# dt's two nine-row matmuls read copies at partitions 0 and 64 and are issued as one step

## The chip, the cores and the metric

The kernel runs on one core of one Trainium2 chip. The metric is the device time in microseconds (us) of one execution, given as the median of several runs. Engines are named as the profile names them: PE (TensorE matmuls), PEld (its weight loads), DVE (VectorE), ACT (ScalarE), POOL (GpSimd) and SP (SyncE, which only issues DMAs here). All data is fp32.

## The reference, cut to what matters

Two graph layers over 4096 nodes with 128 features, each followed by a residual and a layer norm:

```python
h   = relu(adj @ x @ gcn_w + gcn_b); h = layernorm(h) * ln_g + ln_b
xz  = h @ w_in;  xc, z = xz[:, :256], xz[:, 256:]
u   = silu(causal_conv4(xc) + conv_b)
dbc = u @ w_xp                                  # 8 (dt rank) + 16 (B) + 16 (C) columns
dt  = softplus(dbc[:, :8] @ w_dt + b_dt)        # 256 channels
hst = exp(dt*A) * hst + dt * B * u              # scan over 4096 steps, 256 channels x 16 states
y   = (sum_s hst*C + u*D_skip) * silu(z);  x1 = layernorm(x + y @ w_out)
# second layer: two three-layer MLPs, on adj @ x1 and on adj @ x2, merged by Wm
out = layernorm(x1 + concat(mlp1(2*adj@x1), mlp2(2*adj@x2)) @ Wm.T + bm)
```

What matters here is `dt`: a product over only eight rows (nine with the bias `b_dt` as a ninth row against a row of ones), for 256 channels, that is two groups g = 0 and 1 of 128.

## The kernel before

The 4096 nodes are cut into 8 chunks of 512. Everything is kept transposed, features on partitions and 512 nodes along the free dimension, so nearly every matmul is 128x128 weights by 128x512 moving data; in fp32 each is issued as two weight loads and two passes, and the profile counts both.

TensorE does two kinds of work. The bulk is the adjacency products: `one` blocks (adj @ [x, x2] for a chunk, into banks p_x and p_x2; one tile of a block is two matmuls, four passes) and `two` blocks (adj @ x1, one matmul or two passes a tile, into p_two, later into p_x and p_x2). Each block is 1 MB of adj, loaded by SP into a ring of four. Between the tiles stand the steps of the chain of the next chunk, in a fixed order: `gcn`, `cen`, `var`, `in_x`, `x_proj`, `dt1`, `dt0`, then `z` for the gate, `out`, and the MLP steps `mlp0` to `mlp3`.

A chunk is 16 units (one per state s) of two halves. In a unit ACT computes exp(dt*A) for both groups (L565), DVE scans both (L783) and multiplies by C (L792), and POOL makes dt*u*B two units ahead (L948) and adds the product to y (L957). `chain_steps(c)` (L115) puts TensorE's steps into halves of units: `x_proj` of chunk c+1 into the second half of unit o+4, `dt1` into the first half and `dt0` into the second half of unit o+5, with o = 7, 5, 3, 3, ... (`origin`, L110). `spread_blocks` (L145) then spreads the chunk's adjacency tiles over the 32 halves, so that each half carries the same cost, where a `one` tile costs 2, a `two` tile 1, and a step 1 or what `COST` (L142) says. The tiles keep their order; only how many stand between two steps follows from the costs. Chunk 0's own chain is issued after the ramp, with a list of filler tiles between its steps (`FILL`, L49; loop L514).

The steps in question: `x_proj` (L450) multiplies u by `wx3`, whose 128 columns are zero but for dt's eight at 0 to 7 and B's and C's from 16, so p_m holds dt's rows on partitions 0 to 7. ACT copies p_m's partitions 0 to 63 to `dbc` (L647), adding `one_row`, which is 1 on partition 8 only, and writes B's and C's rows to DRAM, from where they are spread over the partitions. `dt1` (L455) multiplies `dbc[0:9]` with the second 128 columns of `w_dt` into bank p_two, `dt0` (L459) with the first 128 into p_m. Both wait for `s_dbc`. ACT's `softplus` (L650) then takes |.| of both banks (L653) and exp and ln of the two together (L655, L657), DVE finishes dt (L832), and POOL makes dt*u (`dtu`, L965).

Other waits that the prediction speaks of: `take_rows` (L585), where ACT copies p_x and p_x2 out; the step `z`, whose two matmuls ACT copies to `gate` (L629) at unit 0; `out` at DVE's unit 3 and ACT's `x1` behind it (L663); `cen` on TensorE (L428), which waits for ACT's `hr` (L599), queued behind `x1`; and DVE's `add_sum` (L808), which adds a finished `two` sum to acc2, and for which a later sum's bank waits.

Of the kernel before, what the change touches and what calls it, by code (L numbers as in the profile page):

```python
# [5 lines left out]
ALU = mybir.AluOpType  # L6
ACT = mybir.ActivationFunctionType

P = 128
# [7 lines left out]
R = 8  # L17
# [11 lines left out]


ROW_B = 16

PACK = {}
_at = 0
# [80 lines left out]
def chain_steps(c):  # L115

    table = {}

    def put(unit, half, name, n):
        table.setdefault((unit, half), []).append((name, n))  # L120

    put(0, 1, "z", c)
    if c:
        put(2, 0, "out", c - 1)
    at = 2 if c == 0 else 3 if c == 1 else 4 if c == NC - 1 else 12
    put(at, 0, "mlp0", c)
    put(at, 1, "mlp1", c)
    put(at + 1, 0, "mlp2", c)
    put(at + 1, 1, "mlp3", c)
    if c + 1 < NC:  # L130
        o = origin(c)
        put(o, 0, "gcn", c + 1)
        put(o, 1, "cen", c + 1)
        put(o + 1, 0, "var", c + 1)
        put(o + 2, 0, "in_x", c + 1)
        put(o + 4, 1, "x_proj", c + 1)
        put(o + 5, 0, "dt1", c + 1)
        put(o + 5, 1, "dt0", c + 1)
    return table


COST = {"z": 2, "out": 2, "in_x": 2, "x_proj": 2}  # L142


def spread_blocks(c):  # L145
# [43 lines left out]
def two_layer_graph_kernel(nc, blocks, xs_d, pack_d, w_dt_d, eps1_d, eps2_d, bm_d, rows_d, out_d):  # L189
    ctx = ExitStack()  # L190
    with ctx:
# [76 lines left out]
        s_pack, s_wdt, s_consts_in = sem("s_pack"), sem("s_wdt"), sem("s_consts_in")  # L268
        s_xs = [sem(f"s_xs{i}") for i in range(NBLK)]
        s_zero, s_A = sem("s_zero"), sem("s_A")  # L270
        s_mean_w, s_cen_w, s_wx3, s_scales = (sem(n) for n in ("s_mean_w", "s_cen_w", "s_wx3", "s_scales"))
        s_gw, s_bxzp, s_wp, s_win, s_bias = (sem(n) for n in ("s_gw", "s_bxzp", "s_wp", "s_win", "s_bias"))
        s_tile = [sem(f"s_tile{i}") for i in range(JT)]
        s_blk = [sem(f"s_blk{i}") for i in range(RING)]
# [65 lines left out]
        @block.sync  # L340
        def _(sp_):
            def load(i):
                kind, m, k = LOADS[i]
                wait(sp_, s_blk_used, i - RING + 1)
                src = blocks[m, k] if kind == "one" else blocks[k, m]
                sp_.dma_start(ring[:, i % RING, :, :], src).then_inc(s_blk[i % RING], 16)

            for jt in range(JT):
                sp_.dma_start(xs[:, jt, :], xs_d[0, :, jt]).then_inc(s_tile[jt], 16)
                sp_.dma_start(ring[:, 0, jt, :], blocks[0, 0, :, jt]).then_inc(s_tile[jt], 16)  # L350
            for k in range(1, NBLK):
                sp_.dma_start(xs[:, JT * k:JT * (k + 1), :], xs_d[k]).then_inc(s_xs[k], 16)
                load(k)
                if k == 1:
                    sp_.dma_start(pack[:, :], pack_d).then_inc(s_pack, 16)
                if k == 3:
                    sp_.dma_start(w_dt[0:R + 1, :], w_dt_d).then_inc(s_wdt, 16)
                    sp_.dma_start(scale1[:, :], eps1_d).then_inc(s_consts_in, 16)
                    sp_.dma_start(scale2[:, :], eps2_d).then_inc(s_consts_in, 16)
                    sp_.dma_start(bm[:, :], bm_d).then_inc(s_consts_in, 16)  # L360
            for i in range(NBLK, len(LOADS)):
                load(i)
            for k in range(NC):
                sp_.wait_ge(s_fin, k + 1)
                sp_.dma_start(out_d[k], mb4(k % 2)).then_inc(s_out[k % 2], 16)
            for q in range(2):
                sp_.wait_ge(s_out[q], 16 * (NC // 2))

        @block.tensor
        def _(pe):  # L370
# [44 lines left out]
            def step(name, n):  # L415
# [16 lines left out]
                elif name == "in_x":  # L432
                    pe.wait_ge(s_h, n + 1)
                    pe.matmul(p_m[:, :], w_in[:, 0:P], hr[:, :], start=True, stop=True).then_inc(s_xc, 1)

                    wait(pe, s_zcopy, G * n)
                    if n >= 1:
                        pe.wait_ge(s_two_add, 1 + sums_added(n - 1, origin(n - 1) + 2) if n < NC - 1 else TURN + 1)
                    else:
                        pe.wait_ge(s_bias, 1)  # L440
                    pe.matmul(p_two[:, :], w_in[:, P:2 * P], hr[:, :], start=True, stop=True).then_inc(s_xc, 1)
                elif name == "z":

                    pe.wait_ge(s_dt, G * (n + 1))
                    wait(pe, s_res0, n)
                    pe.matmul(p_m[:, :], w_in[:, P * G:P * (G + 1)], hr[:, :], start=True, stop=True).then_inc(s_z, 1)
                    pe.wait_ge(s_two_add, 1 + min(sums_added(n, 1), TURN))
                    pe.matmul(p_two[:, :], w_in[:, P * (G + 1):P * (G + 2)], hr[:, :],
                              start=True, stop=True).then_inc(s_z, 1)
                elif name == "x_proj":  # L450
                    pe.wait_ge(s_u, G * (n + 1))
                    for g in range(G):
                        last = pe.matmul(p_m[:, :], wx3[:, g, :], u[:, g, :], start=g == 0, stop=g == G - 1)  # L453
                    last.then_inc(s_dbcp, 1)
                elif name == "dt1":  # L455
                    pe.wait_ge(s_dbc, n + 1)
                    pe.matmul(p_two[:, :], w_dt[0:R + 1, P:2 * P], dbc[0:R + 1, :],  # L457
                              start=True, stop=True).then_inc(s_dtp, 1)
                elif name == "dt0":  # L459
                    pe.wait_ge(s_dbc, n + 1)  # L460
                    pe.matmul(p_m[:, :], w_dt[0:R + 1, 0:P], dbc[0:R + 1, :],  # L461
                              start=True, stop=True).then_inc(s_dtp, 1)
                elif name == "out":
                    pe.wait_ge(s_yg, n + 1)
                    if n < NC - 1:
                        pe.wait_ge(s_zcopy, G * (n + 1) + 1)
                    else:
                        pe.wait_ge(s_res0, NC)
                    for t in range(JT):
                        for g in range(G):  # L470
                            last = pe.matmul(p_m4[:, t, :], y[:, n % 2, g, P * t:P * (t + 1)], w_out[:, g, :],
                                             start=g == 0, stop=g == G - 1)
                    last.then_inc(s_o, 1)
                elif name == "mlp0":
                    pe.wait_ge(s_ax2, n + 1)
                    if n == 0:
                        pe.wait_ge(s_zcopy, 1)
                    elif n == 1 or n == NC - 1:
                        pe.wait_ge(s_r, n)
                    else:  # L480
                        pe.wait_ge(s_dt, G * (n + 2))
                    pe.matmul(p_m[:, :], W2[:, 0, :], ax2[:, n % 2, :], start=True, stop=True).then_inc(s_mm2, 1)
                elif name in ("mlp1", "mlp2"):
                    l = int(name[3])
                    pe.wait_ge(s_mr2, L * n + l)
                    pe.matmul(p_m[:, :], W2[:, l, :], mb[:, (l - 1) % 2, :], start=True, stop=True).then_inc(s_mm2, 1)  # L486
                elif name == "mlp3":
                    pe.wait_ge(s_mr2, L * n + L)
                    for t in range(JT):
                        last = pe.matmul(p_m4[:, t, :], mb[:, 0, P * t:P * (t + 1)], Wm[:, 1, :],  # L490
                                         start=True, stop=True)
                    last.then_inc(s_mm2, 1)
# [16 lines left out]
                    pe.matmul(p_m[:, :], cen_w[:, :], hr[:, :], start=True, stop=True).then_inc(s_wp, 1)  # L509
            pe.wait_ge(s_wx3, 1)  # L510
            pe.wait_ge(s_mean_w, 1)
            pe.wait_ge(s_wdt, 16)
            tile = 0
            for name in ("gcn", "cen", "var", "in_x", "x_proj", "dt1", "dt0"):  # L514
                step(name, 0)
                for _ in range(FILL.get(name, FILL["dt"] if name == "dt0" else 0)):
                    one(NBLK + tile // JT, tile % JT, tile % JT + 1)
                    tile += 1
            assert tile == JT * len(FILL_BLOCKS)
# [38 lines left out]
        def _(act):  # L558
# [35 lines left out]
            def step(name, n):  # L594
# [47 lines left out]
                elif name == "x_proj":  # L642
# [1 line left out]
                    wait(act, s_dtp, G * n)  # L644
                    wait(act, s_rows, 16 * n)
                    wait(act, s_x1, n - 1)
                    act.activation(dbc[0:64, :], p_m[0:64, :], ACT.Identity, bias=one_row[0:64, :]).then_inc(s_dbc, 1)  # L647
                    act.wait_ge(s_dbc, n + 1)
                    act.dma_start(rows_d[b], dbc[ROW_B:ROW_B + 2 * S, :]).then_inc(s_rows, 16)
                elif name == "softplus":  # L650
# [290 lines left out]
        def _(pool):  # L941
# [18 lines left out]
            def step(name, n):  # L960
# [9 lines left out]
                elif name == "resid":  # L970
# [10 lines left out]

            pool.affine_select(out=cen_w[:, :], in_=cen_w[:, :], compare_op=ALU.not_equal, fill=1.0 - 1.0 / D,
                               base=0, pattern=[[-1, P]], channel_multiplier=1).then_inc(s_cen_w, 1)
            pool.affine_select(out=one_row[:, :], in_=one_row[:, :], compare_op=ALU.not_equal, fill=1.0,
                               base=-R, pattern=[[0, 1]], channel_multiplier=1)
            pool.memset(mean_w[:, :], 1.0 / D).then_inc(s_mean_w, 1)
            pool.memset(acc2[:, :], 0.0).then_inc(s_two_add, 1)
            pool.wait_ge(s_pack, 16)
            pool.tensor_copy(wx3[:, :, 0:R], w_xp[:, :, 0:R])
            pool.tensor_copy(wx3[:, :, ROW_B:ROW_B + S], w_xp[:, :, R:R + S])  # L990
            pool.tensor_copy(wx3[:, :, ROW_B + S:ROW_B + 2 * S], w_xp[:, :, R + S:R + 2 * S]).then_inc(s_wx3, 1)
            step("dtu", 0)
# [59 lines left out]
```

## Time and profile before

| | |
|---|---|
| median of 3 runs | 875.76 us (872.22 to 877.38) |
| the profiled execution's own time | 871.53 us |
| its span (first to last instruction) | 869.4 us |
| mean granted TensorE clock | 0.981 |
| PE busy | 830.5 us (96%), 2074 records |
| POOL, DVE, ACT busy | 639.6 (74%), 607.8 (70%), 376.2 (43%) |
| HBM | 206.65 MB read, 241 GB/s over the span |

How to read it: PE's records overlap (a pass of 512 columns has a record of 592 ns, but the next one begins 430 ns behind it), so its busy time says that it hardly pauses, not how much it does. What a step costs on PE is read from the starts of its neighbours, or from the chain of work, which cuts the records where the next begins.

### The profile page before, as it was taken

How to read it: one execution, taken by the hardware profiler on the slowest of the kernel's cores; microseconds unless marked ns; L12 is line 12 of the kernel's file. 1: busy time of each engine (PE TensorE's matmuls, PEld its weight loads, DVE VectorE, ACT ScalarE, POOL GpSimd, SP SyncE). 2: the span in 40 equal slices, each digit the busy share in tenths (PEclk: the TensorE clock that was granted, in tenths of full speed). 3: DMA queues.
4: the chain of work that ended last, by engine and by line, in shares of the span. 5: the costliest groups of instructions: out<-in, count | busy, mean ns of one | idle time of the engine just before them, and what ended most of it. 6: DMA issues, size and time to landing. Idle time of an engine off the chain costs nothing.

```text
span 869.4 us, 7245 instructions
## 1 busy us (share of the span) xinstructions
PE 830.5 (96%) x2074; PEld 374.7 (43%) x2074; DVE 607.8 (70%) x826; ACT 376.2 (43%) x605; POOL 639.6 (74%) x292
## 2 busy tenths in 40 slices
PE   7999989998999999989998999899989998999996
PEld 3444434344444444444444444444444443444453
DVE  0002187877887887888778886888688879886147
ACT  0003444546562655356434643464346536321233
POOL 2000399999899989997999799989997999991000
PEclk9999989999999999999999999999999999899998
DMA  8744567675567657865778567857788999796701
GB/s 328 304 145 142 170 208 228 204 261 199 191 202 264 219 193 283 294 244 191 257 246 276 175 247 245 290 190 246 247 327 287 333 373 353 270 400 236 282 28 73
DMA packets 59482, 209.75 MB, mean 241 GB/s; under 512 B 6954, under 2 KB 7603, under 8 KB 43059
## 3 DMA queue, kind: packets, MB, share of 16 engines
q1 hardware_dynamic: 22194, 141.65, 44.3%
q10 hardware_dynamic: 37248, 67.65, 24.1%
q8 instruction: 16, 0.26, 0.1%
q14 instruction: 24, 0.19, 0.1%
HBM read 206.65 MB, written 2.62 MB: 241 GB/s over the span
## 4 chain that ended last, share of the span: by engine, by line
PE 83%; DVE 9%; ACT 3%; issue 2%; POOL 1%; DMA 1%; ACTq 0%; DVEq 0%; SPq 0%
PE p_x L380 46%; PE p_x L399 18%; PE p_two L399 4%; DVE p_h L783 4%; PE p_m L486 2%; PE p_m L453 2%; DVE prod L792 2%; PE p_dA L555 1%; PE p_m L428 1%; DVE bn L813 1%; PE p_two L457 1%; DVE nmean L842 1%; PE p_m L461 1%; ACT x L678 1%; PE p_m L431 1%
## 5 line engine op out<-in xcount | busy, mean ns | idle before, releaser
L380 PE MATMUL p_x<-ring,xs 128*128 128x512 f32 x1024 | 459.5, 601 | 7.1 <-DMA ring<-adj_blocks 5.8
L957 POOL TENSOR_TENSOR y<-y,prod 128x1024 f32<-128x1024 f32 x127 | 298.8, 2353 | 48.6 <-DVE prod L792 48.5
L380 PEld LDWEIGHTS p_x<-ring,xs 128*128 128x128 f32 x1024 | 194.6, 192 | 255.6 <-issue 249.5
L948 POOL TENSOR_TENSOR bh<-spread,dtu 128x1024 f32<-128x1024 f32 x128 | 301.7, 2357 | 2.7 <-DMA spread<-bc_rows 2.5
L783 DVE TENSOR_TENSOR_SCAN p_h<-p_dA,state,bh 128x512 f32<-128x512 f32 x224 | 276.2, 1279 | 37.5 <-ACT p_dA L565 30.0
L565 ACT ACTIVATE p_dA<-dt,A 128x512 f32<-128x512 f32 x256 | 171.6, 689 | 144.2 <-DVE p_h L783 140.1
L399 PE MATMUL p_x<-ring,x 128*128 128x512 f32 x384 | 174.3, 605 | 2.3 <-issue 2.3
L792 DVE TENSOR_TENSOR prod<-p_h,spread_C 128x1024 f32<-128x1024 f32 x128 | 155.3, 1213 | 0.0
L399 PEld LDWEIGHTS p_x<-ring,x 128*128 128x128 f32 x384 | 73.8, 194 | 96.5 <-issue 96.5
L965 POOL TENSOR_TENSOR dtu<-dt,u 128x1024 f32<-128x1024 f32 x8 | 18.8, 2353 | 84.8 <-DVE dt L832 84.8
L399 PE MATMUL p_two<-ring,x 128*128 128x512 f32 x128 | 58.5, 592 | 0.0
L808 DVE TENSOR_TENSOR acc<-p_x,acc 128x512 f32<-128x512 f32 x32 | 21.9, 684 | 42.9 <-PE p_x L399 42.9
L783 DVE TENSOR_TENSOR_SCAN p_h<-p_dA,bh 128x512 f32<-128x512 f32 x32 | 37.5, 1218 | 13.4 <-POOL bh L948 6.2
L399 PEld LDWEIGHTS p_two<-ring,x 128*128 128x128 f32 x128 | 24.1, 190 | 29.2 <-issue 29.2
L826 DVE TENSOR_TENSOR hr<-hr,p_m 128x512 f32<-128x512 f32 x8 | 5.5, 688 | 36.8 <-ACT p_m L608 36.5
L801 DVE SCALAR_TENSOR_TENSOR p_m<-xcv,pack,p_m 128x512 f32<-128x512 f32 x24 | 18.1, 755 | 15.4 <-ACT p_m L623 14.9
L791 DVE COPY state<-p_h 128x2 f32<-128x2 f32 x128 | 19.8, 155 | 11.9 <-DMA spread_C<-bc_rows 2.5
L486 PE MATMUL p_m<-mb,pack 128*128 128x512 f32 x32 | 18.6, 666 | 9.3 <-ACT mb L684 9.3
L832 DVE SCALAR_TENSOR_TENSOR dt<-p_two,dt 128x512 f32<-128x512 f32 x8 | 5.5, 692 | 28.4 <-ACT dt L657 28.4
L589 ACT ACTIVATE ax<-p_x 128x512 f32<-128x512 f32 x8 | 4.8, 597 | 42.4 <-PE p_x L380 42.4
L684 ACT ACTIVATE mb<-p_m,pack 128x512 f32<-128x512 f32 x16 | 11.0, 689 | 24.0 <-PE p_m L486 24.0
L428 PE MATMUL p_m<-hr,cen_w 128*128 128x512 f32 x16 | 9.6, 682 | 11.4 <-ACT hr L599 11.4
(116 smaller groups left out, 552.2 us busy)
## 6 DMA issues: line engine op xcount, KB each, us to landing
ring<-adj_blocks SPq DMA_DIRECT2D x127, 1024.0 KB, 6.0
spread<-bc_rows ACTq DMA_DIRECT2D x128, 256.0 KB, 4.1
spread_C<-bc_rows ACTq DMA_DIRECT2D x128, 256.0 KB, 5.0
xs<-xs_tiles SPq DMA_DIRECT2D x7, 512.0 KB, 12.8
out_tiles<-mb SPq DMA_DIRECT2D x8, 256.0 KB, 2.0
pack<-pack_w SPq DMA_DIRECT2D x1, 1026.5 KB, 11.3
ring<-adj_blocks SPq DMA_DIRECT2D x4, 256.0 KB, 4.6
xs<-xs_tiles SPq DMA_DIRECT2D x4, 128.0 KB, 4.0
```

The costliest lines, as they stand in the source:

```text
L380: last = pe.matmul(bank[:, :], xs[:, j, D * half:D * (half + 1)], ring[:, i % RING, jt, :], start=j == 0, stop=j == N // P - 1)
L399: last = pe.matmul(sum_bank(i)[:, :], x1[:, m % KEEP, jt, :], ring[:, i % RING, jt, :], start=jt == 0 and opens(i), stop=jt == JT - 1 and ...
L428: pe.matmul(p_m[:, :], cen_w[:, :], hr[:, :], start=True, stop=True).then_inc(s_cen, 1)
L486: pe.matmul(p_m[:, :], W2[:, l, :], mb[:, (l - 1) % 2, :], start=True, stop=True).then_inc(s_mm2, 1)
L565: act.activation(p_dA[g][:, :], dt_[:, c % 2, g, :], ACT.Exp, scale=A[:, g, unit:unit + 1]).then_inc(s_dA, 1)
L783: dve.tensor_tensor_scan(p_h[:, g, :], p_dA[g][:, :], bh[:, i % 3, g, :], first, ALU.mult, ALU.add).then_inc(s_scan, 1)
L791: dve.tensor_copy(state[:, unit, :], p_h[:, :, T - 1]).then_inc(s_state, 1)
L792: dve.tensor_tensor(prod[:, i % 2, :, :], p_h[:, :, :], both(spread_C[:, i % SLOTS_C, :]), ALU.mult).then_inc(s_cmul, 1)
L808: dve.tensor_tensor(acc2[:, T * k:T * (k + 1)], sum_bank(i)[:, :], acc2[:, T * k:T * (k + 1)], ALU.add).then_inc(s_two_add, 1)
L948: pool.tensor_tensor(bh[:, i % 3, :, :], both(spread[:, i % SLOTS, :]), dtu[:, c % 2, :, :], ALU.mult).then_inc(s_bmul, 1)
L957: pool.tensor_tensor(y[:, c % 2, :, :], y[:, c % 2, :, :], prod[:, i % 2, :, :], ALU.add).then_inc(s_acc, 1)
L965: pool.tensor_tensor(dtu[:, b, :, :], dt_[:, b, :, :], u[:, :, :], ALU.mult).then_inc(s_dtu, 1)
```

## The change

`dt1` and `dt0` become one step `dt` in the first half of unit o+5 with a cost of 1 (in all 1 less per chunk than before). Its two matmuls are issued directly behind each other: group 1 reads partitions 0 to 8 of `dbc` and `w_dt`, group 0 partitions 64 to 72. For that `wx3` has dt's eight columns twice (at 0 and at 64), ACT's eviction covers all 128 partitions, `one_row` has a second one on partition 72, and `w_dt` is loaded twice. The placement of tiles by `spread_blocks` follows the new costs; the rest of the kernel is as before.

```diff
+ROW_DT = (0, 64)
...
-        put(o + 5, 0, "dt1", c + 1)
-        put(o + 5, 1, "dt0", c + 1)
+        put(o + 5, 0, "dt", c + 1)
...
-COST = {"z": 2, "out": 2, "in_x": 2, "x_proj": 2}
+COST = {"z": 2, "out": 2, "in_x": 2, "x_proj": 2, "dt": 1}
...
-                    sp_.dma_start(w_dt[0:R + 1, :], w_dt_d).then_inc(s_wdt, 16)
+                    for row in ROW_DT:
+                        sp_.dma_start(w_dt[row:row + R + 1, :], w_dt_d).then_inc(s_wdt, 16)
...
-                elif name == "dt1":
+                elif name == "dt":
+
                     pe.wait_ge(s_dbc, n + 1)
-                    pe.matmul(p_two[:, :], w_dt[0:R + 1, P:2 * P], dbc[0:R + 1, :],
-                              start=True, stop=True).then_inc(s_dtp, 1)
-                elif name == "dt0":
-                    pe.wait_ge(s_dbc, n + 1)
-                    pe.matmul(p_m[:, :], w_dt[0:R + 1, 0:P], dbc[0:R + 1, :],
-                              start=True, stop=True).then_inc(s_dtp, 1)
+                    for g, bank in ((1, p_two), (0, p_m)):
+                        rows = slice(ROW_DT[g], ROW_DT[g] + R + 1)
+                        pe.matmul(bank[:, :], w_dt[rows, P * g:P * (g + 1)], dbc[rows, :],
+                                  start=True, stop=True).then_inc(s_dtp, 1)
...
-            pe.wait_ge(s_wdt, 16)
+            pe.wait_ge(s_wdt, 32)
...
-            for name in ("gcn", "cen", "var", "in_x", "x_proj", "dt1", "dt0"):
+            for name in ("gcn", "cen", "var", "in_x", "x_proj", "dt"):
                 step(name, 0)
-                for _ in range(FILL.get(name, FILL["dt"] if name == "dt0" else 0)):
+                for _ in range(FILL[name]):
...
-                    act.activation(dbc[0:64, :], p_m[0:64, :], ACT.Identity, bias=one_row[0:64, :]).then_inc(s_dbc, 1)
+                    act.activation(dbc[:, :], p_m[:, :], ACT.Identity, bias=one_row[:, :]).then_inc(s_dbc, 1)
...
-            pool.affine_select(out=one_row[:, :], in_=one_row[:, :], compare_op=ALU.not_equal, fill=1.0,
-                               base=-R, pattern=[[0, 1]], channel_multiplier=1)
+            for q, row in enumerate(ROW_DT):
+                wait(pool, s_one_row, q)
+                pool.affine_select(out=one_row[:, :], in_=one_row[:, :], compare_op=ALU.not_equal, fill=1.0,
+                                   base=-(row + R), pattern=[[0, 1]], channel_multiplier=1).then_inc(s_one_row, 1)
...
-            pool.tensor_copy(wx3[:, :, 0:R], w_xp[:, :, 0:R])
+            for row in ROW_DT:
+                pool.tensor_copy(wx3[:, :, row:row + R], w_xp[:, :, 0:R])
```

## Rows read from the trace of the kernel before

**Rows 1.** The page, part 1: busy us, share of the span, instructions.
```profile
PE 830.5 (96%) x2074; PEld 374.7 (43%) x2074; DVE 607.8 (70%) x826; ACT 376.2 (43%) x605; POOL 639.6 (74%) x292
```

**Rows 2.** The page, part 4: the chain that ended last, by engine.
```profile
PE 83%; DVE 9%; ACT 3%; issue 2%; POOL 1%; DMA 1%; ACTq 0%; DVEq 0%; SPq 0%
```

**Rows 3.** Waits of PE: us in total, times, longest.
```profile
PE p_m L428 <- ACT hr L599: 11.4, 5, 2.5
PE p_m L486 <- ACT mb L684: 9.3, 3, 4.3
```

**Rows 4.** Stretches: engine busy us (instructions), clock, DMA; one chunk's length.
```profile
412.00:500.00 88.00, 85.55 (x212) 38.25 (x210) 70.69 (x87) 43.42 (x70) 79.49 (x35) 0.98 0.70 239
```

**Rows 5.** The chain in order of time, start us and us, around one dt.
```profile
407.10 1.72 PE p_m L453 x4
408.82 1.72 PE p_x L380 x4
410.54 1.05 PE p_two L457 x2
411.59 1.91 PE p_x L380 x4
413.50 1.05 PE p_m L461 x2
414.55 13.93 PE p_x L380 x32
```

**Rows 6.** Timeline of chunk 0's dt: start, us, instruction, [idle before <-releaser].
```profile
94.91 0.29 PEld L457 LDWEIGHTS p_two<-dbc,w_dt 9*128 9x128 f32 x2 [0.76 <-issue]
94.91 1.12 PE L457 MATMUL p_two<-dbc,w_dt 9*128 9x512 f32 x2
95.45 0.18 PEld L461 LDWEIGHTS p_m<-dbc,w_dt 9*128 9x128 f32 x1 [0.24 <-issue]
95.87 1.02 PE L461 MATMUL p_m<-dbc,w_dt 9*128 9x512 f32 x2
...
96.82 0.30 PEld L380 LDWEIGHTS p_x<-ring,xs 128*128 128x128 f32 x2 [0.76 <-issue]
...
96.93 0.60 ACT L653 ACTIVATE dt<-p_m 128x512 f32<-128x512 f32 x1 [0.26 <-PE p_m L461]
```

**Rows 7.** Timeline of chunk 1's dt, issued in chunk 0.
```profile
168.81 0.68 ACT L647 ACTIVATE dbc<-p_m,one_row 64x512 f32<-64x512 f32 x1 [3.05 <-PE p_m L453]
...
169.55 1.12 PE L457 MATMUL p_two<-dbc,w_dt 9*128 9x512 f32 x2 [0.77 <-ACT dbc L647]
```

**Rows 8.** Timeline around the step z of chunk 5.
```profile
539.31 2.35 POOL L969 TENSOR_TENSOR y<-y,gate 128x1024 f32<-128x1024 f32 x1
...
542.46 2.47 DVE L783 TENSOR_TENSOR_SCAN p_h<-p_dA,state,bh 128x512 f32<-128x512 f32 x2 [2.62 <-ACT p_dA L565]
...
544.38 1.02 PE L446 MATMUL p_m<-hr,pack 128*128 128x512 f32 x2
...
545.50 0.69 ACT L629 ACTIVATE gate<-p_m,b_xz 128x512 f32<-128x512 f32 x1 [2.56 <-PE p_m L446]
```

**Rows 9.** Timeline of chunks 6 and 7: x_proj's eviction, and waits for sums.
```profile
672.57 1.88 PE L399 MATMUL p_x<-ring,x 128*128 128x512 f32 x4
...
672.77 0.68 ACT L647 ACTIVATE dbc<-p_m,one_row 64x512 f32<-64x512 f32 x1 [1.44 <-PE p_m L453]
...
716.50 0.69 DVE L808 TENSOR_TENSOR acc<-p_x,acc 128x512 f32<-128x512 f32 x1 [2.37 <-PE p_x L399]
...
784.79 12.32 PE L399 MATMUL p_x<-ring,x 128*128 128x512 f32 x24 [2.03 <-issue]
```

**Rows 10.** The chain behind one wait of L428.
```profile
384.54 1.13 PE p_m L428 x2
385.67 3.22 PE p_x L380 x4
```

**Rows 11.** Timeline of POOL behind the kernel's start.
```profile
101.11 2.34 POOL L965 TENSOR_TENSOR dtu<-dt,u 128x1024 f32<-128x1024 f32 x1 [83.63 <-DVE dt L832]
```

More of the change, by code:

```diff
@@ L270, in two_layer_graph_kernel @@
         s_zero, s_A = sem("s_zero"), sem("s_A")
-        s_mean_w, s_cen_w, s_wx3, s_scales = (sem(n) for n in ("s_mean_w", "s_cen_w", "s_wx3", "s_scales"))
+        s_mean_w, s_cen_w, s_wx3, s_scales, s_one_row = (sem(n) for n in (
+            "s_mean_w", "s_cen_w", "s_wx3", "s_scales", "s_one_row"))
         s_gw, s_bxzp, s_wp, s_win, s_bias = (sem(n) for n in ("s_gw", "s_bxzp", "s_wp", "s_win", "s_bias"))
```

## The prediction

> **What bounds the kernel now.** I read the page's busy shares first: PE 96%, POOL 74%, DVE 70% [rows 1]. PE's records overlap, so the share alone proves nothing; the chain that ended last does: 83% of it is PE [rows 2]. Then the waits of PE: behind the start it waits for others in only two places that repeat, `cen` (L428) for ACT's `hr`, five times and 11.4 us in all, and the MLP steps (L486) for ACT, 9.3 us [rows 3]. The rest of the time it streams tiles, one pass every 0.43 us. So a microsecond that PE doesn't need is a microsecond of the kernel, if the other engines can follow. POOL is the next in line: in the 88 us of one chunk it is busy 79.5 [rows 4], 8.5 us of slack.
>
> The chain shows what one dt costs [rows 5]. Two plain tiles (four passes) take 1.72 us, so a pass takes 0.43 and a matmul of two passes 0.86. But `dt1` takes 1.05, the four passes behind it 1.91, and `dt0` 1.05 again. Entering a nine-row matmul costs 0.19 us above its passes, and so does leaving it. Rows 6 show the same in the weight loads: the first nine-row load stands 0.76 us behind the one before it instead of 0.24, likewise the first 128-row load behind the pair. Between `dt1` and `dt0`, which stand side by side there, the gap is 0.24: from one nine-row matmul to the next nothing is paid. That is a price per change between full and nine-row matmuls: four a chunk where tiles stand between the two halves of dt, two where none do.
>
> **The change part by part.** dt runs eight times: once in the prologue, and for chunks 1 to 7 inside the chunks.
>
> 1. *Two changes of shape fewer.* For chunks 1 to 7 the two matmuls now stand together, with one entry and one exit: 2 x 0.19 = 0.38 us less each [rows 5], 7 x 0.38 = 2.66 us. The prologue had them together already, nothing there. Bounds: if going from partition 0 to 64 costs as much as a change of shape, 0.19 of it stays, 1.3 us in all; above, 2.66.
>
> The Trainium skill (TensorEngine Tiling (Array Packing), Key Properties) says that changing the tiling mode drains TensorE and changing only the tile does not. The 0.19 us agree with the first half; for the second, no row here has a matmul at partition 64.
>
> 2. *The two side by side.* No row shows two matmuls at different partitions, so bounds: none of it overlaps, 0; or `dt0` vanishes wholly behind `dt1`, 0.86 us a chunk. What rows 6 show is the order: load, pass, load, pass for `dt1`, then the same for `dt0`, each pass 0.43 behind the last, in the order of issue. `dt1`'s second pass needs the same rows of the array as its first, so it can't start before the first has streamed; `dt0`'s first pass stands behind it in the queue. If order of start is kept and only the rows differ, pass 1 of `dt1` runs alone, its pass 2 beside pass 1 of `dt0`, then pass 2 of `dt0` alone: three times 0.43 instead of four. I take this middle, 0.43 us a chunk, 7 x 0.43 = 3.0 us; it is the value that the observed order of issue gives. Ends: 0 and 6.0.
>
> The Trainium skill (TensorE: Matmul & The Clock Gate, Part 3) has matmuls in different row groups start about 4 ns apart, and all of them starting and ending in program order. Read for single passes the first would hide all of `dt0`; with the second, and two passes each, one of four is hidden. No run here shows either yet.
>
> 3. *A wait in chunk 0.* TensorE waited 0.77 us for ACT's eviction there, because no tile stood between `x_proj` and `dt1` [rows 7]. Working `spread_blocks` with one less cost in the chunk, the half of `x_proj` gets one `one` tile (1.72 us), taken from the halves ahead. ACT's eviction takes 0.68 us and PE waited 0.77 for it, so a tile of 1.72 covers it: 0.77 us gained. Elsewhere the placement hardly moves: tiles shift by half a unit where no step lies between, so PE's order is the same, no sum and no `take_rows` changes its unit. Only in chunk 6 one `two` tile (0.86 us) is left between `x_proj` and `dt` instead of two. There ACT has `dbc` at 672.77 + 0.68 = 673.45 [rows 9], and with one tile less PE would reach the load at 674.38 - 0.86 = 673.52: covered by 0.07, a stall of 0 to 0.1.
>
> 4. *The prologue.* Here the chain goes from `dt` through ACT, DVE and POOL. ACT's second |.| waited 0.26 for `dt0` [rows 6]; with `dt0` 0.43 earlier that wait is gone and ACT's own first |.| is late next: 0.25 us gained, nothing if point 2 gives nothing. PE's own 0.43 there goes into its later wait at L486 (4.3 us) [rows 3].
>
> 5. *Costs.* Eviction of 128 instead of 64 partitions: 0.68 us for 64x512 in rows 7, 0.69 for 128x512 in rows 8: nothing, 0.01 a chunk at most. The second load of `w_dt`, one DMA issue on SP in the ramp ahead of the later ring loads, is hidden by the ring of four; without cover one issue, some 0.4 us. POOL's extra select and copy stand before an idle time of 83.6 us [rows 11]; uncovered they would be under 0.4. `dt0` half a unit earlier adds no wait: both matmuls wait for the same `dbc`, and behind them are only tiles, already loaded. For ACT it removes a wait of about 2.4 us in front of the second |.|, which ACT and DVE turn into idle time elsewhere, as they are not the bound there.
>
> **Does it reach the end?** A chunk's gain sits at unit 8 and must pass the gate at `z`. There ACT waits 2.56 us for PE, DVE idles 2.62, and POOL had its `gate_y` done at 541.7 for a `z` at 544.4 [rows 8]: all three are ahead of PE by more than the 0.8 us that one chunk gives, and behind the gate everything starts from there, the 2.4 us wait at L428 included, which stays as long. In chunk 6 DVE waits 2.37 us for PE's sum [rows 9], so the last gain passes too. In chunk 7 PE waits 2.03 us for a DVE sum ending at 784.79 [rows 9], but DVE's stretch starts from PE's sum, so both move.
>
> Sum: 2.66 + 3.0 + 0.77 + 0.25 = 6.7 us. The profiled execution took 871.53 us with a span of 869.4; it would take 864.8. The median of the runs is 875.76, 4.2 above it, with 872.22 to 877.38 for the three runs; the same subtraction gives 869.1.
>
> **The rivals.**
>
> *No overlap.* The matmuls are beside each other in the program but not in the array: what is left is 2.66 + 0.77 = 3.4 us, 872.4. For it: nothing in the trace overlaps two passes; fp32's two passes each may hold the array. Against: different rows and different banks leave nothing to share but the queue.
>
> *Full overlap.* `dt0` starts with `dt1`: 2.66 + 6.0 + 0.77 + 0.25 = 9.7 us, 866.1. Against it the order of issue in rows 6.
>
> *The gain is swallowed.* POOL has 8.5 us slack in a chunk, but runs without a pause for long stretches, so DVE may give back what PE gains, and PE waits longer at L428 or for sums. Then 0 to 1 us is left: 875.3. Against it the idle times at the gate.
>
> *Slower, by the clock.* Behind a wait PE sometimes runs at the lower clock: four passes took 3.22 us instead of 1.72 after the wait ending at 384.54 [rows 10], a granted clock near half, 1.5 us lost. Of the like waits some are followed by it and some are not. If the shifted times made every one of the seven waits of rows 3 fall, and half of them for eight passes, that adds 2 x 1.5 + 4 x 1.5 = 9 us, against a gain of 3.4 to 6.7: about +4, 880. It decides from three more such stretches than now without overlap, five with it. Against it: the waits keep their length, and where the fall lands looks like chance already in before.
>
> **How the numbers follow.** Half overlap 0.47, none 0.25, full 0.13, swallowed 0.08, slower 0.07. The predicted time is that of half overlap, 869.1. The range goes from below full overlap less a scatter of 2 us (864) to between none and swallowed (874). 0.5% is 4.4 us, about what a measurement of this kernel can tell from no change. Half overlap is beyond it by 2.3 us, with scatter 0.85 of its cases; full nearly always; no overlap 0.25 of its cases: 0.40 + 0.13 + 0.06, so 0.60 faster. Slower by over 0.5% 0.05. The rest, 0.35, is no change.
>
> **What would show it.** In the profile after: the first nine-row load with a gap of 0.76 and the first full load behind with the same, once a chunk instead of twice (step 1). The time from the first pass of the tile before dt to the first pass behind it: 4 x 0.43 + 0.38 = 2.1 us means no overlap, 1.7 half, 1.2 full; and in the chain the starts of the two matmuls' records (step 2). No wait of L457's successor for `dbc` at about 168 us (step 3). ACT's second |.| without a wait at 97 us (step 4). Starts of L428 and `z` earlier by about 0.8 us more in every chunk, with L428's waits still about 2.4 us each. Wrong would be: L428's waits longer by the gain; more than five stretches of doubled passes; or PE's time at dt unchanged.

## The result and the profile after

| | before | after |
|---|---|---|
| median of the runs | 875.89 us (871.96 to 877.48, 6 runs) | 862.43 us (861.4 to 867.19, 6 runs) |
| profiled execution: time, span | 871.53, 869.4 | 861.8, 859.8 |
| mean granted clock | 0.981 | 0.987 |

The ratio is 0.9863, 95% interval [0.9829, 0.9896]. It goes with the means of the runs, 863.1 and 875.1 us, which lie 12.0 us apart; the medians lie 13.5 us apart, the two profiled executions 9.7. The forecast was 869.1 with a range of 864.0 to 874.0, so the kernel came out faster than its lower end.

The page of after, parts 1 and 4 (busy shares; the chain by engine), as in [rows 1, 2]: the bound is still PE.

```profile
PE 817.4 (95%) x2074; PEld 371.2 (43%) x2074; DVE 609.6 (71%) x826; ACT 374.5 (44%) x605; POOL 639.7 (74%) x294
...
PE 82%; DVE 10%; ACT 3%; issue 2%; POOL 1%; DMA 1%; ACTq 0%; DVEq 0%; SPq 0%
```

One thing first on which partitions are which. In the line `rows = slice(ROW_DT[g], ...)` with `ROW_DT = (0, 64)`, it is group 1, issued first and into p_two, that reads partitions 64 to 72, and group 0 that reads 0 to 8; the description of the change has the two the other way round. The two groups of rows differ either way, so the argument stands.

The chain of after around the dt whose counterpart stands in [rows 5] (start us, us):

```profile
405.64 1.72 PE p_m L455 x4
407.36 1.72 PE p_x L382 x4
409.07 0.62 PE p_two L462
409.70 0.01 PE p_m L462
409.70 0.42 PE p_two L462
410.12 0.01 PE p_m L462
410.13 15.65 PE p_x L382 x36
```

The whole of dt takes 0.62 + 0.01 + 0.42 + 0.01 = 1.06 us ahead of the next tile, where before it took 1.05 twice and 0.19 in the tile between: 1.23 us less (1.24 by the rounded terms of the prediction, 0.86 + 0.38). The timeline of an earlier dt of after shows why (start, us, instruction, [idle]):

```profile
247.70 0.18 PEld L462 LDWEIGHTS p_two<-dbc,w_dt 9*128 9x128 f32 x1 [0.76 <-issue]
247.70 0.69 PE L462 MATMUL p_two<-dbc,w_dt 9*128 9x512 f32 x1
247.71 0.18 PEld L462 LDWEIGHTS p_m<-dbc,w_dt 9*128 9x128 f32 x1
247.71 0.69 PE L462 MATMUL p_m<-dbc,w_dt 9*128 9x512 f32 x1
247.81 0.18 PEld L462 LDWEIGHTS p_two<-dbc,w_dt 9*128 9x128 f32 x1
247.81 0.18 PEld L462 LDWEIGHTS p_m<-dbc,w_dt 9*128 9x128 f32 x1
248.23 0.59 PE L462 MATMUL p_two<-dbc,w_dt 9*128 9x512 f32 x1
248.24 0.59 PE L462 MATMUL p_m<-dbc,w_dt 9*128 9x512 f32 x1
248.76 0.30 PEld L382 LDWEIGHTS p_x<-ring,xs 128*128 128x128 f32 x2 [0.76 <-issue]
```

Both first passes start within 0.01 us, both second passes too: `dt0` vanishes wholly behind `dt1`, its weight loads included. The gap of 0.76 us stands once ahead of the pair and once behind it; between partition 64 and partition 0 there is none. The start-to-start distance from the first pass of the pair to the first load behind it is 1.06 us, for `dt1` alone it was 674.38 to 675.43, 1.05.

Where the time went by chunk. The figures are the distances between the starts of successive `x_proj` steps, in us:

| from x_proj of chunk | 0 | 1 | 2 | 3 | 4 | 5 | 6 |
|---|---|---|---|---|---|---|---|
| before | 77.22 | 75.75 | 75.76 | 88.54 | 88.56 | 86.84 | 88.51 |
| after | 73.96 | 79.93 | 75.73 | 85.58 | 85.55 | 85.56 | 85.58 |

From chunk 3 on, after needs 85.57 each time. Before needs 86.84 once, 1.27 more: the 1.23 of the chain, 0.20 by a shorter wait of L428 (2.43 us there, 2.23 in after), less 0.16, because in after two passes of tiles take 0.51 and 0.50 us from start to start instead of 0.43 (those begun at 449.3 and 449.8 us, and at 534.8 and 535.3). And before needs about 88.54 three times, another 1.7 more. Chunk 0 gave 3.3: the 1.23, the wait of 0.77, and a low-clock stretch less (1.7), against another wait that is 0.5 longer. Chunk 2 gave nothing and chunk 1 lost 4.2. Both remainders are what the experiments are about. First the 1.7. These rows of before are the stretches behind two of the waits of L428 (columns: stretch, length, busy us of PE, PEld, DVE, ACT, POOL, granted clock, DMA share, GB/s):

```profile
386.00:390.00 4.00, 4.00 (x7) 1.73 (x6) 2.75 (x3) 1.52 (x4) 4.00 (x3) 0.61 0.65 242
...
474.00:478.00 4.00, 4.00 (x7) 1.62 (x6) 3.28 (x3) 1.79 (x3) 4.00 (x3) 0.57 0.71 262
```

And the same places of after, behind the same step:

```profile
384.00:388.00 4.00, 3.23 (x8) 1.55 (x9) 3.29 (x5) 2.51 (x5) 4.00 (x3) 1.00 0.84 310
470.00:474.00 4.00, 3.67 (x9) 1.76 (x10) 3.29 (x6) 2.06 (x4) 4.00 (x3) 1.00 0.87 322
556.00:560.00 4.00, 4.00 (x10) 1.85 (x11) 3.29 (x5) 2.16 (x4) 4.00 (x2) 1.00 0.82 299
642.00:646.00 4.00, 4.00 (x11) 1.85 (x10) 3.29 (x5) 2.56 (x5) 4.00 (x3) 1.00 0.81 309
```

Before had three stretches at the lower of the two clock levels (1.2 instead of 2.4 GHz) behind its four waits of L428 in chunks 3 to 6, each worth 1.7 us (88.54 against 86.84); after had none there. In chunk 1 it was the other way round: after had two such stretches behind a wait of L487 (208.9 us), before had none; with a wait 1.9 us longer (2.82 us) that makes the 4.2 lost, less what the pair gave. That wait was longer because of one small DVE instruction, seen here in before, and then in after:

```profile
205.97 0.17 DVE L842 TENSOR_SCALAR nmean<-mv 128x4 f32<-128x4 f32 x1
...
202.67 2.35 POOL L958 TENSOR_TENSOR y<-y,prod 128x1024 f32<-128x1024 f32 x1
202.95 2.09 DVE L843 TENSOR_SCALAR nmean<-mv 128x4 f32<-128x4 f32 x1
```

It makes four columns and lasts 2.09 us, until POOL's instruction ends (205.02). In before it took 0.17 at this place, because it fell where POOL's instruction was just ending. It stands between the statistics and x1, and so ahead of `hr` and of the waits of L428 and L487 (L430 and L487 in after, L428 and L486 in before). The wait in chunk 1 follows it: 0.91 us in before, 2.82 in after; in e1, e8 and e4 nmean takes 1.53, 1.99 and 2.22 us there and the wait lasts 2.25, 2.72 and 2.95.

### The profile page after: what moved, and what is told of

Same layout as the page of the kernel before. It is cut to its first block, busy times and chain, and to the rows that moved or that the text cites. A ratio compares the mean times of both kernels' runs of the same rounds, so it can differ in the third digit from the quotient of the medians.

```text
span 859.8 us, 7249 instructions
## 1 busy us (share of the span) xinstructions
PE 817.4 (95%) x2074; PEld 371.2 (43%) x2074; DVE 609.6 (71%) x826; ACT 374.5 (44%) x605; POOL 639.7 (74%) x294
## 4 chain that ended last, share of the span: by engine, by line
PE 82%; DVE 10%; ACT 3%; issue 2%; POOL 1%; DMA 1%; ACTq 0%; DVEq 0%; SPq 0%
PE p_x L382 46%; PE p_x L401 18%; PE p_two L401 4%; DVE p_h L784 4%; PE p_m L487 2%; PE p_m L455 2%; DVE prod L793 2%; PE p_dA L556 1%; DVE nmean L843 1%; DVE bn L814 1%; PE p_two L462 1%; PE p_m L430 1%; ACT x L679 1%; PE p_m L491 1%; PE p_m L433 1%
## 5 line engine op out<-in xcount | busy, mean ns | idle before, releaser
L401 PE MATMUL p_x<-ring,x 128*128 128x512 f32 x384 | 172.0, 600 | 3.6 <-issue 3.6
L487 PE MATMUL p_m<-mb,pack 128*128 128x512 f32 x32 | 19.4, 693 | 11.7 <-ACT mb L685 11.7
L802 DVE SCALAR_TENSOR_TENSOR p_m<-xcv,pack,p_m 128x512 f32<-128x512 f32 x24 | 18.1, 755 | 15.4 <-ACT p_m L624 14.8
L809 DVE TENSOR_TENSOR acc<-p_two,acc 128x512 f32<-128x512 f32 x8 | 5.5, 685 | 22.7 <-PE p_two L401 22.7
L430 PE MATMUL p_m<-hr,cen_w 128*128 128x512 f32 x16 | 8.7, 625 | 11.7 <-ACT hr L600 11.7
```

Source lines behind the costliest of these rows:

```text
L401: last = pe.matmul(sum_bank(i)[:, :], x1[:, m % KEEP, jt, :], ring[:, i % RING, jt, :], start=jt == 0 and opens(i), stop=jt == JT - 1 and ...
L802: dve.scalar_tensor_tensor(out=bank[:, :], in0=xcv[:, g, k:k + T], scalar=conv_w[:, g, k:k + 1], in1=bank[:, :], op0=ALU.mult, op1=ALU.add ...
L809: dve.tensor_tensor(acc2[:, T * k:T * (k + 1)], sum_bank(i)[:, :], acc2[:, T * k:T * (k + 1)], ALU.add).then_inc(s_two_add, 1)
```

## The experiments

e1 to e4, e5 to e8, and e9 to e11 each ran side by side with the kernel before; their ratios are to it.

**e1, both matmuls on the same rows.** One entry and one exit, but no overlap.

```diff
-                        rows = slice(ROW_DT[g], ROW_DT[g] + R + 1)
+                        rows = slice(0, R + 1)
```

> The changed kernel, but both nine-row matmuls of a pair read partitions 0 to 8; the copies at 64 are made and not used. If the rows are what lets the two run together (theory), the pair costs again four passes and one entry and exit, 1.72 + 0.38 = 2.10 us instead of 1.24: 7 x 0.86 = 6.0 us more than the changed kernel, and about 3.4 us (0.4%) less than the kernel before. If the gain came from the placement (one entry and exit, the tile in chunk 0, less wait on ACT) and not from the overlap (rival), it stays within 1.5 us of the changed kernel.

Measured: 870.95 us, ratio 0.9931 [0.9907, 0.9955]. The chain of this kernel:

```profile
323.78 1.72 PE p_x L382 x4
325.50 1.05 PE p_two L462 x2
326.55 0.86 PE p_m L462 x2
327.40 2.77 PE p_x L382 x6
```

Four passes, one entry: the pair takes 1.91 us ahead of the exit, 0.85 more than in after. So it is the rows that let the two run together; the two banks differ here as well, and alone they do not do it. The distance to the changed kernel (0.9863 against 0.9931) is 0.7%, 6 us, as the theory had it (8.5 us between the medians, which come from different comparisons); placement alone is out as the source of the whole. Against before it gained 6 us where 3.4 were expected; the clock has a part in that, as the ledger below shows.

**e4, the copies without the pair.** The matmul on partitions 0 to 8 stands half a unit behind the one on 64 to 72.

```diff
-        put(o + 5, 0, "dt", c + 1)
+        put(o + 5, 0, "dt1", c + 1)
+        put(o + 5, 1, "dt0", c + 1)
...
-                    for g, bank in ((1, p_two), (0, p_m)):
+                    for g, bank in {"dt1": ((1, p_two),), "dt0": ((0, p_m),)}[name]:
```

> The changed kernel's copies at partitions 0 and 64, but the two matmuls in separate halves of the unit with tiles between them, as in the kernel before (only in the prologue do they stand together). If all comes from standing side by side (theory), this is the kernel before in time, within 0.3%, with 1.05 us for each and 0.19 us more behind each; if partition 64 or the wider eviction changes something by itself (rival), it differs, and the one at 64 has another duration than the one at 0.

Measured: 875.76 us, ratio 0.9984 [0.9956, 1.0011]. The two matmuls, on partitions 64 to 72 and then on 0 to 8, last the same:

```profile
249.67 1.12 PE L462 MATMUL p_two<-dbc,w_dt 9*128 9x512 f32 x2
...
252.64 1.12 PE L462 MATMUL p_m<-dbc,w_dt 9*128 9x512 f32 x2
```

So the copies, the wider eviction and the second load cost nothing that shows, and partition 64 is as good as 0: from `x_proj` to `x_proj` chunks 3 to 6 take 88.51 to 88.55 us, as the disturbed ones of before do. All of the gain comes with the one step: the overlap, the entry and exit saved, and the tile ahead of it in chunk 0, where this kernel waits 0.78 us for `dbc` again. All four of this kernel's waits of L428 from chunk 3 on were followed by the lower clock, as here:

```profile
388.00:392.00 4.00, 3.96 (x6) 1.68 (x7) 2.39 (x5) 1.79 (x3) 4.00 (x2) 0.57 0.75 282
```

**e8, partitions 96 and 64.**

```diff
-ROW_DT = (0, 64)
+ROW_DT = (96, 64)
```

> The changed kernel with group 0 at partitions 96 to 104 and group 1 at 64 to 72, next to each other and in turned order. If any two different groups of rows run together (theory), both first passes start within 0.02 us and the time is that of the changed kernel, 862 us. If the two must lie in different halves of the array (rival), the pair takes four passes and the kernel 6 us more.

Measured: 863.34 us, ratio 0.9868 [0.9818, 0.9918], the changed kernel's time. The first dt's first passes start at 94.48 and 94.49, the second ones both at 95.02. Neighbouring groups of 32 rows run together as well.

**e2 and e3, nmean as a tensor_tensor**, in the kernel before and in the changed one; `neg` is a new tile that holds -1.

```diff
-                    dve.tensor_scalar(nmean[:, :], mv[:, b, :, 0], -1.0, None, ALU.mult).then_inc(s_stats, 1)
+                    dve.tensor_tensor(nmean[:, :], mv[:, b, :, 0], neg[:, :], ALU.mult).then_inc(s_stats, 1)
```

> The kernel before, with one DVE instruction of another form: nmean (L842) as a tensor_tensor with a tile of -1 instead of a tensor_scalar. In both profiles the tensor_scalar of 128x4 elements takes 0.17 to 2.10 us and ends where POOL's running instruction ends. If its form is what waits for POOL (theory), it takes under 0.2 us here, x1 and hr come 1 to 1.7 us earlier in each of the seven chunks, the waits of L428 shrink from 2.4 to about 0.9 us, with no stretch at the lower clock behind them, and the kernel is 8 to 14 us faster than before. If any DVE write or read there waits for POOL (rival), nothing changes.

> The changed kernel with the same new form of nmean. If the change itself is worth 9.5 us (full overlap 6.0, two changes of shape less 2.7, the wait in chunk 0 0.8) and the rest of the measured 13.5 us is where POOL's phase and the lower clock happened to fall (theory), this kernel is 9 to 10 us faster than the kernel before with the same new form, and both show the same number of low-clock stretches. If the change is worth more than its passes by something of its own (rival), the difference between the two stays at 13 us.

Measured: e2 876.44 us, 1.0001 [0.9975, 1.0027]; e3 864.26 us, 0.9851 [0.9813, 0.9888]. A miss: the new form waits as long.

```profile
381.10 1.76 DVE L843 TENSOR_TENSOR nmean<-mv,neg 128x4 f32<-128x4 f32 x1
...
386.62 1.95 PE L429 MATMUL p_m<-hr,cen_w 128*128 128x512 f32 x2 [2.40 <-ACT hr L600]
```

The form is not what waits, so the comparison that e3 was made for was not had: the two are 12.2 us apart, and their traces hold nine and seven low-clock stretches ahead of the kernel's end, not the same number. Both are repeats of their originals, which still says something: the changed kernel's lead came back, 1.5% here and 1.4% before.

**e5, e6 and e7, nmean on ACT**, in the kernel before, the changed one, and e1.

```diff
-                    act.wait_ge(s_stats, 2 * (n + 1))
+                    act.wait_ge(s_aggr, n + 1)
                     act.activation(rstd[:, b, :], mv[:, b, :, 1], ACT.Ln, bias=eps_t[:, :]).then_inc(s_rv, 1)
+                    act.activation(nmean[:, :], mv[:, b, :, 0], ACT.Copy, scale=-1.0).then_inc(s_stats, 1)
...
                     act.wait_ge(s_rv, 2 * n + 2)
+                    act.wait_ge(s_stats, 2 * (n + 1))
...
-                    dve.wait_ge(s_aggr, n + 1)
-                    dve.tensor_scalar(nmean[:, :], mv[:, b, :, 0], -1.0, None, ALU.mult).then_inc(s_stats, 1)
```

> The kernel before, with nmean made by ACT behind its Ln instead of by DVE, so that no DVE instruction with both ends in SBUF stands between the statistics and x1. If the 1 to 2 us of nmean are a wait for POOL (theory), they go: hr comes 1 to 1.7 us earlier, L428 waits 0.8 to 1.2 instead of 2.4 us, no stretch at the lower clock follows, and from x_proj to x_proj every chunk from the third takes 85.3 to 85.8 us instead of 86.8 or 88.5; in all 10 to 15 us less than before, and less scatter between runs. If they are DVE's own work on four columns of statistics (rival), ACT takes as long and nothing is gained.

> The changed kernel with the same edit. If the change is worth the passes and changes of shape that it removes and the rest was the fall of the clock (theory), its chunks take 1.24 us less than those of the kernel before with the edit, and the two differ by 8.5 to 9.5 us, not by 13.5. If the change has a further effect of its own (rival), the difference stays above 12 us. It should be the fastest of all, near 852 us.

> Both matmuls of a pair on partitions 0 to 8, with the same edit to nmean. Chunks 0.86 us longer than with the copies at 64 and 0.38 us shorter than the kernel before with the edit (theory): 6 us above the former, 3 to 3.5 below the latter. If the low clock alone made the difference between same rows and copies (rival), it disappears here.

| | median us | ratio to before | x_proj to x_proj, chunks 3 to 6 |
|---|---|---|---|
| e5, dt apart | 856.32 | 0.9789 [0.9749, 0.9828] | 85.01, 85.01, 85.01, 85.05 |
| e7, together, same rows | 854.09 | 0.9765 [0.9723, 0.9807] | 84.62, 84.78, 84.78, 84.93 |
| e6, together, rows 0 and 64 | 846.14 | 0.9677 [0.9638, 0.9717] | 83.76, 83.93, 83.93, 84.07 |

The 1 to 2 us were a wait for POOL: the work takes ACT 0.19 us in all eight places, whatever POOL does. In e5, while POOL runs, ACT makes nmean in 0.19 us, and L428 waits 0.6 us instead of 2.4:

```profile
290.96 2.37 POOL L948 TENSOR_TENSOR bh<-spread,dtu 128x1024 f32<-128x1024 f32 x1
...
292.50 0.19 ACT L666 ACTIVATE nmean<-mv 128x4 f32<-128x4 f32 x1
...
296.02 1.13 PE L428 MATMUL p_m<-hr,cen_w 128*128 128x512 f32 x2 [0.60 <-ACT hr L599]
```

None of those waits is followed by the lower clock in any of the three, and their chunks repeat within 0.3 us. With that noise gone the overlap is 84.78 - 83.93 = 0.85 us a chunk, two passes. Standing together is 85.01 - 84.62 = 0.39 in the first of the four distances, as in the chain, and 0.23 in the next two: there e7 and e6 have the two slower passes of tiles that after has (in e7 at 444.9 and 445.4 us, 0.51 instead of 0.43), and none of the kernels with dt apart has them. What makes them slower is not shown.

The forecasts for e5 were too cautious: L428 waits 0.6 us and not 0.8 to 1.2, a chunk takes 85.01 us and not 85.3 to 85.8 (1.83 less than the undisturbed one of before, which is the wait's 2.43 - 0.60), and the median is 20.4 us below before's and not 10 to 15. e6 came out at 846 and not near 852. The medians of e5 and e6 are 10.2 us apart, between the theory's 9.5 and the rival's 12; e7 and e6 are 8.0 apart where 6.0 were expected, e5 and e7 2.2 where 3 to 3.5 were. Their traces still differ in low-clock stretches in chunk 7, behind waits of PE for the MLP and for sums: e7 three, e5 two, e6 none.

**e9, e10 and e11, the MLP steps of chunks 0 and 7 two units later** on top of e6, e7 and e5.

```diff
-    at = 2 if c == 0 else 3 if c == 1 else 4 if c == NC - 1 else 12
+    at = 4 if c == 0 else 3 if c == 1 else 6 if c == NC - 1 else 12
```

The line stands in three places, for PE, ACT and DVE, and is changed in each.

> The changed kernel with nmean on ACT, and the MLP steps of chunks 0 and 7 two units later (units 4 and 6 instead of 2 and 4), where ACT is no longer stuck between PE's first and second MLP matmul, so that the last long waits of PE (4.7 us in chunk 0, about 4 in chunk 7) and the lower clock behind them go. Theory: 3 to 6 us less than without the delay, near 842 us, with at most two low-clock stretches of 1.7 us in the whole trace.

> The same with both matmuls of a pair on partitions 0 to 8. With the clock falls gone from both kernels, the overlap is worth 7 x 0.86 = 6.0 us (theory); if the overlap does more than hide two passes (rival), the difference stays at the 8 us seen between the medians with the falls in.

> The kernel before with both edits (nmean on ACT, MLP steps of chunks 0 and 7 later). Theory: 7 x 1.24 + 0.8 = 9.5 us above the changed kernel with both edits, and 3.5 us above the one with both matmuls on the same rows. If the low clock at these waits made part of the 10.2 us between the kernels with nmean alone (rival to an effect of the pair itself), the difference comes down from 10.2 towards 9.5.

| | median us | ratio to before |
|---|---|---|
| e11, dt apart | 852.07 | 0.9737 [0.9702, 0.9772] |
| e10, together, same rows | 849.36 | 0.9717 [0.9682, 0.9751] |
| e9, together, rows 0 and 64 | 844.35 | 0.9656 [0.9624, 0.9689] |

The overlap is now worth 5.0 us by the medians (expected 6.0), the whole change 7.7 (expected 9.5), e10 against e11 2.7 (expected 3.5); 7 x 1.08, the difference between the chunks of e5 and e6, is 7.6. The step from 10.2 to 7.7 is within the scatter of the runs, so by itself it doesn't show the clock's part. The granted clocks of all runs say more. (1 - clock) x span, what the lower clock took from TensorE, averages 8.5, 9.5 and 6.6 us in e5, e7 and e6, and 5.2, 5.6 and 6.7 in e11, e10 and e9. Taken off the means of the runs, the whole change is worth 7.8 us in the first three kernels and 9.3 in the last three, the overlap alone 4.8 and 6.4. That is an estimate, and its scatter covers the 9.5 and 6.0 of the theory.

e9 is the fastest kernel of the study, 3.4% below the one before; of that a quarter to a third is the change this document is about. e9 gained 1.8 us over e6, where 3 to 6 were expected: the wait in chunk 0 fell from 4.7 to 2.3 us, but did not go (3.8 in e10 and 3.0 in e11), and the one in chunk 7 stayed (2.4 in e6, 2.6 in e9).

**The ledger between the two profiled kernels.** Passes and changes of shape: 7 x 1.24 = 8.7 us. The wait in chunk 0: 0.8. Low-clock stretches at 1.7 us each: eight in before and five in after, beside one in each at the very end where it costs nothing, so about 5 us less. Against it nmean: the seven instances inside the chunks sum to 10.0 us in before and 12.4 in after, 2.3 more; and the ramp, where after reaches its first `x_proj` 0.6 us later. 8.7 + 0.8 + 5 - 2.3 - 0.6 = 11.6, against 9.6 measured in the spans. The other 2 us can be found to within 0.4: PE's wait for the MLP in chunk 0 is 4.74 us instead of 4.26, its waits for DVE's sums in chunk 7 are 0.57 and 3.02 instead of 0.31 and 2.03, and seven passes of tiles in chunks 2 to 6 are 0.08 slower each: 0.5 + 1.3 + 0.6 = 2.4.

The difference between all runs (12.0 us by the means, 13.5 by the medians) is larger because this execution of before was one of its luckier ones. In chunks 3 to 6, of the 12 waits of L428 in the three traces with dt apart (before, e2, e4), 11 were followed by the lower clock; of the 12 in the three with the overlap (after, e3, e8), 2; in e1, 2 of 4. That is about three stretches, 5 us, an execution. The waits are 2.40 to 2.45 us in the former and 2.12 to 2.44 in the latter. Removing them (e5 to e7) removed the falls. All runs bear this out, and not only the profiled ones: (1 - clock) x span averages 17.9 us in the 28 runs of before beside e1 to e4 (the stretch at the end, which costs nothing, is in every figure), 18.0 in e2 and 18.4 in e4; 12.3, 12.2 and 11.8 in after, e3 and e8; 14.8 in e1. So the falls give the changed kernel 5 to 6 us over the one before, and e1 3 of the 6 that it gained. That they made the surplus over the passes is shown by that; why they come less often with the shorter chunk is not.

## Why the prediction was wrong

1. *Two changes of shape fewer.* Right: 0.38 us in the chain, and going from partition 64 to 0 costs nothing. By the trace of e1 against the undisturbed chunk of before it is 0.43, of which 0.04 is a shorter wait of L428; with nmean on ACT it is 0.39, and 0.23 where the slower passes of tiles take 0.16 back.
2. *The two side by side.* This is the step that failed. I took 0.43 us a chunk, "the value that the observed order of issue gives"; it measured 0.85, the upper end, 6.0 us in all instead of 3.0. The rows I argued from showed the order of passes on the same nine rows, and said nothing of two groups of rows. Only passes on the same rows follow one another: the program has `dt1` whole ahead of `dt0`, and yet the first pass of `dt0` starts 0.52 us ahead of the second of `dt1`. Whether the engine or the order of the issued loads and passes brings that about, no run shows. The Trainium skill (TensorE: Matmul & The Clock Gate, Part 3) has matmuls in different row groups start about 4 ns apart; at 0.01 us the trace agrees, for each of the two passes. I had weighed its other sentence, on starting and ending in program order, against it, and read it pass by pass. The trace agrees with it for whole matmuls (`dt1` starts and ends no later than `dt0`) and refutes it for passes. Full overlap had a chance of 0.13.
3. *The wait in chunk 0.* Right: no wait of the pair for `dbc` at 168 us. The stall of up to 0.1 in chunk 6 did not come: one `two` tile stands between, and no wait.
4. *The prologue.* Right in kind, too small: ACT's second |.| starts without a wait, and its exp begins 2.27 us behind the start of dt instead of 2.65, 0.38 gained and not 0.25. But after's ramp was 0.6 us later, more than was gained.
5. *Costs.* Right: e4 shows that nothing of it is to be seen.
6. *Does it reach the end?* Right in chunks 3 to 6. Wrong in chunk 2, where before and after need 75.76 and 75.73: there nmean went from 1.04 to 2.09 us and took the gain. e1, e4 and e8 need 75.74 to 75.76 there too, however dt is arranged; with nmean on ACT the same distance is 74.68 (e5), 74.44 (e7) and 73.59 (e6), and the gain is back. In chunk 7, where I had let DVE's stretch move with PE, PE's waits for sums grew by 1.3 us. I had read the 2.4 us wait of L428 as a fixed length; it hangs on POOL's phase. It is the swallowed gain of the rivals, in chunk 2 and by one instruction.
7. *The clock.* I had it only as a rival to the slow side. In the sum it stood at nothing. It moved the other way, by three stretches or 5 us, and with point 2 this put the time under the range. The full-overlap case gave 866.1, inside the range; the measured 862.4 needs the clock too. That this term fell on the fast side was not foreseen by anything in the prediction. (The sum of that rival speaks of seven waits of [rows 3]; the rows count eight, five and three.)

## What to carry to other kernels

Two small matmuls on different groups of 32 rows and into different banks cost one, if nothing stands between them: 1.06 us and 0.19 for the exit here. Apart they cost twice their passes plus twice the entry and exit, 2.5 us. Different rows into the same bank, or more than two at once, no run tried. Count the entries and exits first: they are there in the old trace. And where PE waits 2 us at fixed places, price the clock on both sides of zero, or take the wait away: here that was worth more than the change itself.

## What the runs showed that I had not expected

- Entering or leaving a nine-row matmul from or to full ones costs 0.19 us each; changing from rows 64 to 0 or 64 to 96, nothing.
- fp32's two passes each overlap pair by pair, starts 0.00 to 0.01 us apart, and so do the starts of their weight loads.
- A DVE instruction of 128x4 elements from and to SBUF, in either form (tensor_scalar, tensor_tensor), took from 0.16 to 2.2 us. Whenever POOL was running, it ended within 0.1 us of POOL's instruction (49 instances in seven traces), while statistics and aggregates next to it (0.87 and 0.38 us for four) were not held. On ACT the same work took 0.19 us, and moving it gave 2.1% of the kernel before and 1.9% of the changed one.
- The low clock comes in stretches worth 1.7 us; waits of 0.6 us of PE at the same place were never followed by one (30 waits in e5 to e7 and e9 to e11).
